# Attention over four PSUM score banks, with probabilities turned in place, value strips and tokens two pairs ahead

## The reference, cut to what matters

```python
h = tok(x)                                   # 16 x 256 x 256 -> 16 x 128 x 256
h = h + attn0(layernorm(h))                  # 16 heads of 16, causal window of 64
h = h + ffn0(layernorm(h))                   # 16 experts, top 2, and a shared MLP
h = h + attn1(layernorm(h))                  # 16 heads of 16, causal
return h + ffn1(layernorm(h))                # 64 experts, top 3

# tok: two neighbouring rows k = 0, 1 make one token
x = einsum('btki,oik->bto', xb, conv_w) + conv_b
x = x + xb.mean(axis=2)
x = (x - mean) * rsqrt(var + 1e-5) * ln_gamma + ln_beta
# attention, each head
scores = q @ k.T / 4, masked;  attn = softmax(scores);  out = (attn @ v) @ Wo
```

## Time and profile before

| what | value |
|---|---|
| median of the runs (lowest, highest) | 1438.44 us (1435.76, 1448.89) |
| profiled execution | 1449.65 us |
| its span in the trace, mean granted clock | 1447.9 us, 0.949 |
| PE, DVE, ACT, POOL busy | 92%, 34%, 38%, 23% |

### The profile page before, as it was taken

How to read it: one execution, slowest core, us unless ns; L and a number is a source line. 1 busy time by engine, 2 the same in 40 slices (tenths; PEclk the granted TensorE clock), 3 DMA queues, 4 the chain that set the end, 5 groups by cost and what they waited for, 6 DMA issues and landing times.

```text
span 1447.9 us, 25242 instructions
## 1 busy us (share of the span) xinstructions
PE 1329.1 (92%) x7488; PEld 1086.0 (75%) x7488; DVE 498.5 (34%) x2628; ACT 544.0 (38%) x1928; POOL 332.6 (23%) x327
## 2 busy tenths in 40 slices
PE   5899999986899999979999998299999999999996
PEld 4677777773466666547777776199999999999995
DVE  4355665543122222233555554212221221222121
ACT  1666665661111111035666665033223322322331
POOL 3123333222023333300222222312212212221221
PEclk8899999998999999989999998599999999999998
DMA  9700000001245555451000000279999999999993
GB/s 333 295 16 30 29 29 29 15 13 40 87 108 135 136 116 134 80 192 57 22 16 9 8 7 8 84 229 306 302 309 316 302 303 317 308 300 309 315 301 76
DMA packets 148813, 218.01 MB, mean 151 GB/s; under 512 B 9603, under 2 KB 117093, under 8 KB 148736
## 3 DMA queue, kind: packets, MB, share of 16 engines
q1 hardware_dynamic: 129824, 197.18, 40.3%
q0 software_dynamic: 18944, 20.28, 8.4%
HBM read 178.51 MB, written 45.19 MB: 155 GB/s over the span
## 4 chain that ended last, share of the span: by engine, by line
PE 79%; DVE 5%; issue 5%; ACT 4%; DMA 4%; POOL 2%; SPq 0%; POOLq 0%; DVEq 0%; ACTq 0%
PE bank L1084 16%; PE bank L1097 15%; PE bank L801 8%; PE bank L826 6%; PE bank L1025 5%; PE bank L779 4%; PE bank L811 4%; PE bank L982 3%; PE bank L1036 3%; ACT probs L1168 2%; PE bank L871 2%; PE bank L760 2%; PE bank L1099 2%; DMA early<-rows 2%; PE bank L992 2%
## 5 line engine op out<-in xcount | busy, mean ns | idle before, releaser
L1320 ACT ACTIVATE dhidT<-bank,b1T 128x128 f32<-128x128 f32 x512 | 146.0, 368 | 335.6 <-PE bank L1084 335.5
L1084 PE MATMUL bank<-probsT,arena 128*128 128x128 f32 x2048 | 241.2, 276 | 0.0
L1084 PEld LDWEIGHTS bank<-probsT,arena 128*128 128x128 f32 x2048 | 235.8, 193 | 0.5 <-DVE probsT L1706 0.4
L1097 PE MATMUL bank<-arena,dhidT 128*128 128x256 f32 x1024 | 231.6, 379 | 0.0
L1097 PEld LDWEIGHTS bank<-arena,dhidT 128*128 128x128 f32 x1024 | 189.8, 190 | 23.2
L1168 ACT ACTIVATE probs<-probs,neg_max 128x128 f32<-128x128 f32 x512 | 197.9, 390 | 10.7 <-DVE neg_max L1420 10.5
L704 POOL DMA_INDIRECT stream<-probsT,slot_token x64 | 98.6, 1540 | 403.0 <-DMA stream<-probsT,slot_token 352.9
L1727 DVE TENSOR_SCALAR probsT<-bank,slot_gate 128x256 f32<-128x256 f32 x64 | 30.9, 483 | 384.9 <-PE bank L1099 384.9
L1420 DVE CUSTOM_DVE_ANT_0 probs<-bank,mask 128x128 f32<-128x128 f32 x512 | 117.8, 286 | 121.9 <-PE bank L801 120.8
L801 PE MATMUL bank<-kT,qT 32*128 32x256 f32 x512 | 144.8, 408 | 4.5 <-DVE neg_max L1420 2.1
L826 PE MATMUL bank<-probsT,v_wide 128*128 128x128 f32 x1024 | 140.6, 283 | 1.5 <-ACT probsT L1177 1.3
(11 more groups left out here) (164 smaller groups left out, 1446.3 us busy)
## 6 DMA issues: line engine op xcount, KB each, us to landing
arena<-L_ffn_w SPq DMA_DIRECT2D x128, 1024.0 KB, 7.2
rows<-zeros SPq DMA_DIRECT2D x13, 1024.0 KB, 14.0
drows<-rows SPq DMA_DIRECT2D x64, 132.0 KB, 7.8
arena<-L_ffn_w_gate SPq DMA_DIRECT2D x16, 352.0 KB, 3.7
arena<-L_ffn_w_up SPq DMA_DIRECT2D x16, 352.0 KB, 4.4
early<-rows SPq DMA_DIRECT2D x16, 264.0 KB, 2.7
early<-x SPq DMA_DIRECT2D x8, 512.0 KB, 3.7
arena<-L_ffn_w_down SPq DMA_DIRECT2D x16, 256.0 KB, 3.4
```

The costliest lines, as they stand in the source:

```text
L1084: mm = pe.matmul(bank[2 + 2 * (u % 2) + half][:, jj * P:(jj + 1) * P], w1_sb[u][:, c, j * P:(j + 1) * P], drowsT[:, u % 2, c, :], start=c ...
L1097: pe.matmul(bank[6 + u % 2][:, 0:D], dhidT[:, u % 2, j, :], w2_sb[u][:, j, :], start=j == 0, stop=False)
L1320: last_ = act.activation(dhidT[:, u % 2, j, :], bank[2 + 2 * (u % 2) + half][:, jj * P:(jj + 1) * P], ACT.Gelu, bias=b1T[:, j, bass.ds(e, 1)])
```

## The change

1. Four score banks. `score_bank` is banks 0 to 3; the turn banks are gone. `scores(L, i, t)` writes all four groups of a half at once, in the order m outer, b inner, so that neighbouring matmuls use different 32-row strips and different banks. It has one semaphore increment for the half, and waits until all four groups of the half before have been copied to `probsT`.
2. In-place transposes. `turn_probs` writes the transposed probabilities of group b into score bank b, where DVE has read the scores.
3. Strips. `v_pad` has 32 columns for a head (its 16 and 16 zeros) in place of 128, and the output of group b is the 32 partitions 32b to 32b+31 of `mix_bank`. `values(L, i, t)` does a whole half, again with b inner, after all four groups are turned.
4. Early tokens. `turn_x`, `conv` and the token statistics are done two pairs ahead and split over the pair. The mean of the two rows is folded into the conv weights once (0.5 times the identity added), so `sum_x` on POOL and one DVE pass over the tokens go.
5. A new order of work on every engine. The helpers `step` are gone; the orders are written out, the two halves of a pair are each finished within the pair but for `values(i, 1)`, and v is projected at the start of its own pair. The order of jobs in the front and back banks is made by lists (`front_order`, `back_order`).

```diff
-        score_bank, turn_bank, mix_bank = bank[0:2], bank[2:4], bank[4]
+        score_bank, mix_bank = bank[0:4], bank[4]
...
-                wait(pe, L.max_done, 8 * i + 4 * t + b - 1)
-                row = 32 * b
+                wait(pe, L.turned, 8 * i + 4 * t)
                 for m in range(DC):
-                    last = pe.matmul(score_bank[b % 2][:, 2 * m * P:2 * (m + 1) * P], qT[row:row + 32, m, t, :],
-                                     kT[row:row + 32, m, t, :, :], start=True, stop=True)
+                    for b in range(SBANKS):
+                        row = 32 * b
+                        last = pe.matmul(score_bank[b][:, 2 * m * P:2 * (m + 1) * P], qT[row:row + 32, m, t, :],
+                                         kT[row:row + 32, m, t, :, :], start=True, stop=True)
                 last.then_inc(L.score_full, 1)
...
-                    last = pe.transpose(turn_bank[b % 2][:, j * P:(j + 1) * P], probs[:, t, head(b, j), :], ident[:, :])
+                    last = pe.transpose(score_bank[b][:, j * P:(j + 1) * P], probs[:, t, head(b, j), :], ident[:, :])
...
+                wait(pe, L.turned, 8 * i + 4 * t + SBANKS)
                 for j in range(HEADS_PER_BANK):
-                    m, own = divmod(head(b, j), P // HD)
+                    m, r = divmod(j, 2)
                     col = (2 * m + t) * P
-                    last = pe.matmul(mix_bank[:, col:col + P], v_wide[:, DC * t + m, own * P:(own + 1) * P],
-                                     probsT[:, b, j * P:(j + 1) * P], start=b == 0 and j == 0,
-                                     stop=b == SBANKS - 1 and j % 2 == 1, skip_group_check=True)
+                    for b in range(SBANKS):
+                        own = 2 * b + r
+                        last = pe.matmul(mix_bank[b * STRIP:(b + 1) * STRIP, col:col + P],
+                                         v_pad[:, DC * t + m, own * STRIP:(own + 1) * STRIP], probsT[:, b, j * P:(j + 1) * P],
+                                         start=j == 0, stop=r == 1, skip_group_check=True)
...
+            dve.wait_ge(const_p, 2)
+            dve.wait_ge(prep_free, 2)
+            for k in range(2):
+                for c in range(DC):
+                    own = conv_wT[:, 2 * k + c, c * P:(c + 1) * P]
+                    last = dve.scalar_tensor_tensor(out=own, in0=ident[:, :], scalar=0.5, in1=own, op0=ALU.mult, op1=ALU.add)
+            last.then_inc(conv_ready, 1)
```

The new order of PE in a pair (`now` = pair i, `before_` = i - 1, `ahead` = i + 2, in A only):

```diff
+                    if now:
+                        scores(L, i, 0)
                     if before_:
+                        values(L, i - 1, 1)
                         spread_inverse(L, i - 1)
+                    if there(i - 2, PAIRS):
+                        count(L, i - 2)
+                    if now:
+                        project_v(L, i)
+                        turn_probs(L, i, 0, 0)
                     if before_:
                         project_out(L, i - 1)
                     if now:
+                        turn_probs(L, i, 0, 1)
+                    if ahead:
+                        turn_x(i + 2)
+                    if now:
+                        turn_probs(L, i, 0, 2)
+                        turn_probs(L, i, 0, 3)
+                        scores(L, i, 1)
+                        values(L, i, 0)
+                    if next_:
+                        turn_normed(L, i + 1)
+                    if ahead:
+                        conv(i + 2, 0)
+                    if now:
+                        turn_probs(L, i, 1, 0)
+                    if before_:
+                        turn_ffn_in(L, i - 1)
+                    if next_:
+                        project_qk(L, i + 1, 0)
+                    if before_:
+                        route(L, i - 1)
+                    if now:
+                        turn_probs(L, i, 1, 1)
+                    if next_:
+                        project_qk(L, i + 1, 1)
+                    if now:
+                        turn_probs(L, i, 1, 2)
+                    if ahead:
+                        conv(i + 2, 1)
+                    if now:
+                        turn_probs(L, i, 1, 3)
+                        turn_inverse(L, i)
```

More of the change, by code:

```diff
@@ L79, in loop, with skewed_loop @@
         body(count - 1, False, True)
-def skewed_loop(eng, count, lead, body):
-    for i in range(lead):
+def skewed_loop(eng, count, body):
+    for i in range(2):
         body(i)
-    with eng.Fori(lead, count - 1) as i:
+    with eng.Fori(2, count - 2) as i:
         body(i)
-    for i in range(count - 1, count + lead):
+    for i in range(count - 2, count + 2):
         body(i)
@@ L752, in turn_x, with conv @@
                     last.then_inc(full, 1)
-            def conv(i):
-                for t in range(2):
-                    wait(pe, L0.front_free[t], i * (L0.NF // 2) + 1)
-                    bk, full = front_job(L0, i, 2 + t)
-                    for c in range(2 * DC):
-                        last = pe.matmul(bk[:, 0:D], xT[:, t, c, :], conv_wT[:, c, :], start=c == 0, stop=c == 2 * DC - 1)
-                    last.then_inc(full, 1)
+            def conv(i, t):
+                b, n = front(L0, i, X0 + t)
+                wait(pe, L0.front_free[b], n + 1)
+                bk, full = front_job(L0, i, CONV0 + t)
+                for c in range(2 * DC):
+                    last = pe.matmul(bk[:, 0:D], xT[:, t, c, :], conv_wT[:, c, :], start=c == 0, stop=c == 2 * DC - 1)
+                last.then_inc(full, 1)
             def turn_normed(L, i):
                 wait(pe, L.normed_ready, i + 1)
-                bk, full = front_job(L, i, L.KF)
+                bk, full = front_job(L, i, TURN)
                 for c in range(DC):
@@ L831, in step @@
-            def step(L, s, a, beside):
-                for b in range(SBANKS):
-                    if s:
-                        scores(L, *s, b)
-                    if a:
-                        turn_probs(L, *a, b)
-                        if b >= 1:
-                            values(L, *a, b - 1)
-                    beside(b)
-                if a:
-                    values(L, *a, SBANKS - 1)
+                    for b in range(SBANKS):
[3 more added lines that the diff above has]
+                                         start=j == 0, stop=r == 1, skip_group_check=True)
@@ L1565, in body @@
                     if now:
-                        greatest(L, i, 0, 1)
-                    if now and next_ and L is L1:
-                        front_a(L1, i + 1, False)
-                    if there(i - 2, PAIRS) and L is L1:
-                        weigh(L1, i - 2)
-                    if not now and there(i - 2, PAIRS):
-                        place(L, i - 2)
-                    if not now and before_:
-                        invert(L, i - 1, 1)
-                    if now:
-                        greatest(L, i, 0, 2)
-                        greatest(L, i, 0, 3)
+                        for b in range(1, SBANKS):
+                            greatest(L, i, 0, b)
@@ L1578, in body @@
+                    if next_ and L is L0:
+                        front_b(i + 1)
                     if next_ and L is L1:
-                        front_d(L1, i + 1)
-                    if now and there(i - 2, PAIRS):
-                        place(L, i - 2)
+                        front_c(L1, i + 1)
                     if before_:
                         normalise(L, i - 1)
+                    if there(i - 2, PAIRS):
+                        if L is L1:
+                            weigh(L1, i - 2)
+                        place(L, i - 2)
@@ L1604, in body @@
-                    if next_ and L is L0:
-                        front_d(L0, i + 1)
+                    if ahead:
+                        mix_tokens(i + 2, 0)
                     if before_:
                         choose(L, i - 1)
-                    if before_ and L is L0:
-                        weigh(L0, i - 1)
-                skewed_loop(dve, PAIRS, 2, body)
+                        if L is L0:
+                            weigh(L0, i - 1)
+                    if now:
+                        invert(L, i, 1)
```

375 lines of the change are left out of this document (189 added, 186 removed).

## The result

The changed kernel takes 1393.8 us in the median of 5 runs (1382.1 to 1397.54), the kernel before 1444.97 in 5 beside it (1435.76 to 1448.89). The ratio is 0.9633, 95% interval 0.9596 to 0.9671: 51 us less. The forecast was 1405, laid as 33 us less than 1438.44; against the runs beside it that would be 1412, so 18 us more came than was forecast.

What follows compares the result with a forecast made beforehand. The prediction took PE to set the pace of A and C. A gave -38.5 us and its clock +6.3, C -0.8 in all: sum -33 from 1438.44, so 1405 us, range 1368 to 1456.

Steps and rivals of the forecast that it cites:

- Overlap of the strips: PE in A and C: half the streaming overlaps, scores 2.2 us and values 2.1 a half, saving 7.8 a pair.
- Rival 1: All four strips run at once: scores 1.2 us, values 1.3 a half; 1383 us in all, chance 0.24.
- The chain between halves: Second-half scores wait for the first half's last copy; hand-overs set the pair: 31.3 us in A, 30.9 in C.
- rival 3: No strip overlap: scores 3.9 us, values 4.3 a half; pairs 37 in A, 35 in C; 1474 us, chance 0.14.
- Pair 0: First pair of A: it has no back work and takes 27.5 us.
- The clock: PE falls to half clock after transposes and waits: 0.9 us a pair more in A, 1.7 in C.
- The tails: Ends of A and C: the last ffn input waits for pair 6's scatters, +5.5 us and +5.2.
- The fold: Token work in A: dropping POOL's sums and DVE's pass gives nothing, beyond affine being ready in time.
- B and D: Stages the change only moves; a changed length of either would show the prediction wrong; D keeps 450 of 450.
- Rival 2: Hand-overs each add 0.2 us, or C falls in half its time: +31, 1436 us, no change; chance 0.2.

Runs made afterwards that it cites:

- scores_inner: Changed kernel with the score loops turned inside out, so all matmuls of one strip follow each other; 1389.44 us, 0.961 of the kernel before.
- quad: Changed kernel with each score and value matmul issued four times; 1500.38 us, 1.0387 of the kernel before.
- scores4: Changed kernel with only the score matmuls issued four times; 1477.75 us, 1.02 of the kernel before.
- values4: Changed kernel with only the value matmuls issued four times; 1424.44 us, 0.9828 of the kernel before.
- again: The changed kernel run a second time, unaltered; 1390.72 us, 0.961 of the kernel before.
- warm: Changed kernel with unread full-size matmuls filling idle PE in five places of a pair in C; 1386.9 us, 0.9591 of the kernel before.
- warm_turns: Changed kernel with transposes filling idle PE in five places of a pair in C; 1384.84 us, 0.9571 of the kernel before.
- tail_warm: Changed kernel with transposes as fillers in C and, after the last pair only, count before spread and place before normalise; 1381.99 us, 0.9546 of the kernel before.
- fold_only: Kernel before with only the mean folded into the conv weights, without POOL's sum and one DVE pass; 1442.44 us, 0.9955 of the kernel before.

## Why the forecast held, and where it was wrong

Sign and range were right: 1393.8 for 1405, inside 1368 to 1456. The sum was less good than these two numbers look, since the kernel before took 1444.97 us beside the changed one, not 1438.44: 33 us were forecast and 51 came. A ends 34.0 us sooner for a forecast of 32.2, and that closeness is luck, two errors of opposite sign. C is 22.8 us shorter for a forecast of 0.8, and there no second error hides the first. Step by step, on the profiled executions:

**Overlap of the strips.** Forecast 2.2 and 2.1 us a half; measured 1.08 and 1.01 by pitch. This is the mis-sized term. I had argued that an fp32 matmul is two records in order, so that only half of the streaming overlaps. scores_inner shows that order in the stream doesn't bind row strips. Rival 1 (1.2 and 1.3 us) was the right mechanism. Its pairs of 29.2 in A and 29.8 in C look like those of the chip, 29.0 and 29.3, but they are laid without the clock; with the forecast's charge for it they are 30.1 and 31.5. The fixed part of a visit was taken as 0.3 us, though 4.24 - 3.6 over four visits is 0.16; the measured 1.08 us are 0.86 of streaming, by quad ((3.66 - 1.08) / 3), and 0.2.

The Trainium skill, "TensorEngine Tiling (Array Packing)", Theoretical Speedup, states up to 4x for a dimension of 32 or less; here a half's scores went from 4.24 us to 1.08, 3.9x, which agrees; against their streaming alone, 3.6 us, it is 3.3x. "TensorE: Matmul & The Clock Gate" of the Trainium skill, Part 3, has 3.07x for four row strips; by that I had estimated 1.5 us, and the measurement decides for less. Had I given the page more weight than my argument on records, the forecast would have been rival 1: 55 us less, nearer to the measured 51 than my 33, though without the wait in pair 0.

**The chain between halves.** Right. quad, with the old price and the new chain, gave 37.4 and 35.7 us a pair where rival 3 was laid at 37 and 35. The point from which a pair is as long as before, 6.5 us a half, was right for A and too high for C: a straight line between the pairs of the changed kernel (2.1 us a half for both; 29.0 and 29.3) and of quad (7.3; 36.6 and 35.2) meets those of the kernel before (35.5 and 32.0) at 6.5 and 4.5. By the whole time, with the wait in pair 0 and the tails counted, it is 4.7. Had I weighed the two apart, scores would have had a price of one and values of a third (scores4, values4). Parts 2, 4 and 5 of the change, but for the fold, weren't tried one by one, so what each adds to the chain stays open.

**Pair 0.** Forecast 27.5 us, measured 46.9: a step left out. I laid the next tokens beside pair 0 and never asked what SP's queue has ahead of their load. It costs 19.4 us, and hid the size of the first error: pairs 1 to 6 take 254.08 - 81.46 = 172.6 us against the forecast's 5 x 31.3 + 30.5 + 6.3 of clock = 193.3, 20.7 less. With -0.9 for the start and +0.4 for the end, A is over 1.8 us before the forecast, less than the 3.7 by which A differs in `again`. Reading the row that was to show the step (the starts of scores) is what finds this; the sum alone would have confirmed it. The wait, 20 to 24 us, stands in all twelve traces of kernels with the change. That it would give back its 19 us with the load ahead of the zeros was only argued: it wasn't tried.

**The clock.** Forecast +0.9 us a pair in A and +1.7 in C. Falls in the pair of C that is shown were three, more than nearly two; the granted clock over the stage is 0.80, 0.89 before. But warm and warm_turns undo the fall for 3 to 7 us in C, so the price was half a us to a us a pair, and somewhat more if the fillers cost time. Right in place, too dear in size. C as a whole is 22.8 us shorter for a forecast of 0.8: by `normalise`, 18.8 in the seven pairs (forecast 0, with the clock), 8.4 ahead of the first (forecast 6), less 4.4 in the tail (forecast 5.2). A pair of C was laid at 30.9 + 1.7 = 32.6 us and took 29.3. Of these 3.3 us, 1.1 are the full overlap, as rival 1 lays it, and about 1 is the clock that was too dear; which part of the laying is too long by the last us no run shows.

"TensorE: Matmul & The Clock Gate" of the Trainium skill, Part 4, says that transposes don't count as busy in the way that matmuls do. The falls behind transposes go with it; that transposes as filler raised the clock of C's pairs from 0.85 to 0.96 where matmuls raised it to 0.94 speaks against it, and the measurement decides.

**The tails.** Forecast +5.5 and +5.2; measured 9.9 - 6.1 = 3.8, and 4.4 over C's tail (15.2 - 11.2 = 4.0 to the ffn input). The mechanism, landing scatters ahead of the last ffn input, is in both chains. In tail_warm the old order took about 2 us of it back at either end.

**The fold.** Forecast nothing, since POOL and DVE had idle; some 5 us in the kernel before (fold_only), 3.4 of them seen in A's pairs. In the changed kernel it can't be told from the rest.

**B and D.** D is 507.5 us for 507.6. B differed by 10.9, which the prediction had named as a sign that it is wrong; `again` and the other kernels show that this sign was a bad one, since B moves by as much between executions.

Rival 2 (hand-overs dearer, no gain) is refuted: the pairs are shorter than laid, 29.0 and 29.3 us for 31.3 and 30.9. Rival 3 is refuted as to the change and is what quad does.

## What to carry to other kernels

Where an operand has only 32 rows or columns, putting four such matmuls into different strips was worth nearly four times on PE here (row strips in four banks, column strips in one, both in turn); price it at the full factor, and then lay out the chain of waits that the new order makes, since that and the start, and not PE, took half of it back. When work is moved ahead, follow its operand to the DMA queue: what the queue holds in front of the load was free only as long as the consumer came later. A sum that comes out right is no proof of its terms; read each term's own row.

## What the runs showed of the chip that I had not expected

Four row strips of fp32 matmuls ran at the same time even where the program gives all matmuls of a strip in a row: 0.80 us from first to last start, for 0.77 with the strips in turn. In this TensorE did not do its stream strictly in order. The column strips of the values did so only in part: 2.19 us for 0.81, and 3.43 with four times as many matmuls in turn.

Transposes as filler held PE's granted clock as well as matmuls did (0.96 and 0.94, from 0.85, over C's pairs).

A stage that is the same in two kernels, B, differed by up to 14 us between single profiled executions; the three whose rows stand above have 298.3, 291.4 and 287.4 us at a granted clock of 0.95, 0.97 and 0.99. A profile's stages must be compared with a second profile of the same kernel before a difference in them is explained.
